# Waiting for the gated values block by block in the down projection

## The chip, the core and the metric

The kernel runs on one core of a Trainium2 chip. The metric is the device time of one execution in microseconds. Its reference is a median of three runs.

## The reference

One block with adaptive layer norm: a recurrent attention part with a gated MLP, then a mixture of experts. There are 1024 tokens (4 sequences of 256) of width D = 256. The part around the change is the MLP of the first half:

```
x1n = rmsnorm(x1, norm2_w)
mlp = gelu(x1n @ up1_W + up1_b) * (x1n @ up2_W + up2_b) @ down_W + down_b
return mlp + x1                       # times ga, plus x: this is x2
...
h = layernorm(x2) * (1 + cb) + sb
# router: logits = h @ gate_w, softmax, top 2 of 8 experts
# each expert: gelu(h @ w1[e] + b1[e]) @ w2[e] + b2[e], weighted and summed
```

The MLP is F = 768 wide. The product before `@ down_W`, the gated values, is called v here.

## The kernel before

Everything in the first half is held transposed: features on the 128 partitions, tokens along the free dimension. A tensor of D rows is two blocks of 128 (`KD` = 2), v is six (`KF` = 6). Tokens go in two halves of 512 (`hf` 0 and 1), which is one PSUM bank in float32. The five engines run streams of their own and meet at semaphores; there is no scheduler, the order on each engine is the order of the code. PSUM banks are handed out by a written-out list (`Order.take`); `begin` waits until the bank's former content is drained, `end` counts it as filled.

Products are made with float32 numbers split into a high and a low part, in three matmuls for each pair of blocks (`three`): hi x hi, weight hi x value lo, weight lo x value hi. So one `up` product has 2 x 3 matmuls and one `down` product 6 x 3. `up(hf, m)` makes the two `up` products for block m. Four engines then make the block m of v:

- ACT takes the GELU of `up1` into `g_tile` (`up_gelu`, L1014);
- DVE adds the bias to `up2` and multiplies, into `v_tile` (`v_of`, L1395);
- ACT copies it to `v_hi`, rounded to the format of the products (`v_hi_of`, L1009), and counts `v_hi_done`;
- POOL subtracts it from `v_tile`, which gives `v_lo` (L1652), and counts `v_lo_done`.

Both counts rise by one for each block, six for each half, in the order of the blocks. `v_tile` and `g_tile` have four buffers.

TensorE's order around the change, written out by hand:

```
up(0, 5); up(1, 0); down(0)
up(1, 1); up(1, 2); x2_to_tokens(0)
up(1, 3); up(1, 4); up(1, 5); xhat2_blocks(0)
down(1, [0]); logits(0); to_tokens("h2t", 0, hT); down(1, [1])
places(0); turn_weights(0); x2_to_tokens(1); second_biases(0); stay_busy
xhat2_blocks(1); logits(1); ...
```

`down(hf, dts)` makes the blocks `dts` of the output for a half. DVE turns `down` into x2 (`x2_of`, L1402 and L1408, tile `xT`); TensorE transposes it to tokens (`x2_to_tokens`, L699), DVE takes the layer norm (L1194 to L1205), TensorE transposes back (`xhat2_blocks`, L541), and DVE modulates into `hT` (L1259). `logits` (L718) multiplies this by the router's weights, DVE ranks the experts (`centre`, `choose`), TensorE counts places (`places`, L730 to L735), and DVE makes slots (`slots`). POOL then scatters the tokens' rows to the experts' lists in device memory, SP loads these lists, and the expert loop runs. `x2_of(1)` stands behind `slots(0)` in DVE's code.

In the rows below, L549 is the matmul in `product` (up and down products alike); those that read `v_hi` or `v_lo` belong to `down`.

Of the kernel before, what the change touches and what calls it, by code (L numbers as in the profile page):

```python
# [55 lines left out]
def adaln_block(nc, I, out):  # L56
# [10 lines left out]
    KD, KH, KF, KE = D // P, H // P, F // P, FE // P  # L67
# [112 lines left out]
    with ctx:  # L180
# [11 lines left out]
        def at(name, off, shape, dt=F32):  # L192
            return nc.alloc_sbuf_tensor_at(name, [P, *shape], dt, offset=off)
# [72 lines left out]
        v_hi, v_lo = at("v_hi", o_r1, [KF, T], F32R), at("v_lo", o_r1 + 3 * TB, [KF, T], F32R)  # L266
# [93 lines left out]
        v_hi_done, v_lo_done = sem("v_hi_done"), sem("v_lo_done")  # L360
# [29 lines left out]
        def three(m, n):  # L390

            return ((m[0], n[0]), (m[0], n[1]), (m[1], n[0]))
# [130 lines left out]
        def _(pe):  # L523
            def begin(key):
                b, _, need = order.at[key]
                if need:
                    pe.wait_ge(drained[b], need)
                return b, bank[b]

            def end(ins, b):  # L530
                ins.then_inc(filled[b], 1)
# [12 lines left out]
            def product(key, w, x, k, n=HT):  # L544

                b, ps = begin(key)
                for c in range(k):
                    for t, (l, r) in enumerate(three(w(c), x(c))):
                        ins = nc.tensor.matmul(ps[:, 0:n], l, r, start=(c == 0 and t == 0), stop=(c == k - 1 and t == 2))  # L549
                end(ins, b)  # L550
                return ins
# [59 lines left out]
            def wm(n, k):  # L611
                w = [x[:, n].rearrange("p (k n) -> p k n", k=k) for x in (wm_hi, wm_lo)]
                return lambda m: lambda c: tuple(x[:, c, m * P:(m + 1) * P] for x in w)

            def split_of(hi, lo, hf):
                return lambda c: (hi[:, c, hs[hf]], lo[:, c, hs[hf]])

            def wm_ready(n):
                pe.wait_ge(wm_hi_done, n)
                pe.wait_ge(wm_lo_done, n)  # L620
# [45 lines left out]
            b, ps = begin("gb")  # L666
            for k in range(KD):
                ins = nc.tensor.matmul(ps[0:B, 0:D], cT[:, k, :], wmod_gb[:, k, :], start=(k == 0), stop=(k == KD - 1))
# [15 lines left out]

            def down(hf, dts=range(KD)):
                wm_ready(3)
                pe.wait_ge(v_hi_done, KF * (hf + 1))
                pe.wait_ge(v_lo_done, KF * (hf + 1))
                for dt in dts:
                    product(("down", hf, dt), wm(2, KF)(dt), split_of(v_hi, v_lo, hf), KF)  # L690

            def to_tokens(key, hf, src):

# [72 lines left out]
            up(0, 5)  # L766
            up(1, 0)
            down(0)
            up(1, 1)
            up(1, 2)  # L770
# [3 lines left out]
            up(1, 5)  # L774
            xhat2_blocks(0)
            down(1, [0])
            logits(0)
            to_tokens("h2t", 0, hT)
            down(1, [1])
            places(0)  # L780
            turn_weights(0)
# [86 lines left out]
            with pe.If(ov == 0):  # L868
                for j in range(2):
                    b, _, need = order.at[("rest", j)]  # L870
# [871 lines left out]
```

## Time and profile before

| | us |
|---|---|
| median of three runs | 322.95 |
| lowest, highest | 319.52, 323.54 |
| the profiled execution | 318.49 |
| its span, first to last instruction | 316.7 |
| TensorE busy in it | 273.1 |
| DVE, ACT, POOL busy | 194.7, 180.4, 114.9 |

The profiled execution is one more execution, beside the three. Its time is 1.8 us more than its span; all rows are from it. Busy shares are averages over stages that differ, so they don't tell what a single wait is worth.

### The profile page before, as it was taken

How to read it: one execution, taken by the hardware profiler on the slowest of the kernel's cores; microseconds unless marked ns; L12 is line 12 of the kernel's file. 1: busy time of each engine (PE TensorE's matmuls, PEld its weight loads, DVE VectorE, ACT ScalarE, POOL GpSimd, SP SyncE). 2: the span in 40 equal slices, each digit the busy share in tenths (PEclk: the TensorE clock that was granted, in tenths of full speed). 3: DMA queues.
4: the chain of work that ended last, by engine and by line, in shares of the span. 5: the costliest groups of instructions: out<-in, count | busy, mean ns of one | idle time of the engine just before them, and what ended most of it. 6: DMA issues, size and time to landing. Idle time of an engine off the chain costs nothing.

```text
span 316.7 us, 4350 instructions
## 1 busy us (share of the span) xinstructions
PE 273.1 (86%) x1556; PEld 229.6 (72%) x1556; DVE 194.7 (61%) x450; ACT 180.4 (57%) x290; POOL 114.9 (36%) x97
## 2 busy tenths in 40 slices
PE   0799999958998999686959779999999999999780
PEld 0685446347686888565736669999999999999780
DVE  4766719739645276266495576767676767675520
ACT  5166589762497039251423669494949494949000
POOL 6000000000225033307227530656565656565651
PEclk9999999976999999996656999999999999999997
DMA  7960000000007564602104596393939393917231
GB/s 233 387 185 0 2 1 0 0 0 2 0 0 252 170 161 71 201 0 86 52 19 132 178 274 193 104 288 109 284 111 283 112 283 103 248 17 200 19 45 25
DMA packets 32726, 38.25 MB, mean 121 GB/s; under 512 B 7989, under 2 KB 28333, under 8 KB 32685
## 3 DMA queue, kind: packets, MB, share of 16 engines
q1 hardware_dynamic: 26816, 29.90, 30.0%
q0 software_dynamic: 4928, 7.44, 10.6%
q10 hardware_dynamic: 956, 0.59, 0.6%
q8 instruction: 14, 0.23, 0.3%
q14 instruction: 12, 0.09, 0.1%
HBM read 31.96 MB, written 8.90 MB: 129 GB/s over the span
## 4 chain that ended last, share of the span: by engine, by line
PE 70%; DVE 9%; ACT 8%; issue 6%; DMA 3%; POOL 2%; POOLq 0%; SPq 0%; ACTq 0%; DVEq 0%
PE bank L842 16%; PE bank L864 15%; PE bank L549 14%; PE bank L608 8%; PE bank L560 3%; DMA a_col<-in_L_attn_a_param 2%; PE bank L828 2%; PE bank L568 2%; PE bank L859 2%; PE bank L858 2%; PE bank L541 1%; DVE u L1303 1%; POOL v_lo L1652 1%; PE bank L699 1%; PE bank L753 1%
## 5 line engine op out<-in xcount | busy, mean ns | idle before, releaser
L1704 POOL DMA_INDIRECT out_x<-y_tok,meta x24 | 51.6, 2149 | 50.8 <-DVE y_tok L1576 44.6
L864 PE MATMUL bank<-w_hi,own 128*128 128x256 f32 x256 | 48.0, 286 | 1.8 <-DVE y_tok L1576 1.8
L842 PE MATMUL bank<-xe_hi,w_hi 128*128 128x320 f32 x128 | 39.7, 310 | 3.4 <-DVE xe_lo L1554 3.4
L864 PEld LDWEIGHTS bank<-w_hi,own 128*128 128x128 f32 x256 | 40.4, 191 | 2.4 <-issue 2.0
L1558 DVE TENSOR_TENSOR own<-own_raw,own 128x256 fp32r<-128x256 f32 x64 | 27.2, 425 | 23.5 <-ACT own L1134 18.9
L842 PE MATMUL bank<-xe_lo,w_hi 128*128 128x320 f32 x128 | 39.6, 309 | 0.0
L842 PE MATMUL bank<-xe_hi,w_lo 128*128 128x320 f32 x128 | 39.6, 309 | 0.0
L1128 ACT ACTIVATE own_raw<-bank,b1c 128x320 f32<-128x320 f32 x64 | 33.8, 529 | 8.5 <-PE bank L842 8.4
L864 PE MATMUL bank<-w_lo,own 128*128 128x256 f32 x128 | 36.2, 283 | 0.0
L1134 ACT ACTIVATE own<-own_raw 128x320 fp32r<-128x320 f32 x64 | 28.7, 461 | 0.0
L1695 POOL DMA_INDIRECT gb_rows<-gb_table,meta x24 | 24.4, 1016 | 9.4 <-issue 7.0
L842 PEld LDWEIGHTS bank<-xe_hi,w_hi 128*128 128x128 f32 x128 | 24.0, 188 | 3.7 <-issue 3.7
L864 PEld LDWEIGHTS bank<-w_lo,own 128*128 128x128 f32 x128 | 24.5, 191 | 0.0
L842 PEld LDWEIGHTS bank<-xe_lo,w_hi 128*128 128x128 f32 x128 | 24.0, 188 | 0.0
L842 PEld LDWEIGHTS bank<-xe_hi,w_lo 128*128 128x128 f32 x128 | 24.0, 188 | 0.0
L549 PE MATMUL bank<-n_hi,wm_hi 128*128 128x512 f32 x48 | 20.6, 429 | 3.1 <-DVE n_lo L1286 3.1
L1652 POOL TENSOR_TENSOR v_lo<-tmp,v_hi 128x512 fp32r<-128x512 f32 x6 | 7.7, 1286 | 40.7 <-ACT v_hi L1009 40.7
L1142 ACT ACTIVATE low_rows<-bank 64x256 f32<-64x256 f32 x8 | 3.0, 381 | 34.1 <-PE bank L859 34.1
L549 PE MATMUL bank<-n_lo,wm_hi 128*128 128x512 f32 x48 | 19.5, 407 | 0.0
L549 PE MATMUL bank<-n_hi,wm_lo 128*128 128x512 f32 x48 | 19.5, 405 | 0.0
L1576 DVE SCALAR_TENSOR_TENSOR y_tok<-bank,meta,gb_rows 128x256 f32<-128x256 f32 x16 | 7.7, 484 | 18.1 <-PE bank L864 17.5
L1488 DVE TENSOR_TENSOR w_lo<-e_raw,w_hi 128x2048 fp32r<-128x2048 f32 x8 | 18.6, 2327 | 0.0
(211 smaller groups left out, 614.2 us busy)
## 6 DMA issues: line engine op xcount, KB each, us to landing
e_raw<-in_L_ffn_w SPq DMA_DIRECT2D x16, 1024.0 KB
x_rows<-in_L_attn_x SPq DMA_DIRECT2D x1, 2560.0 KB
xe_tok<-x_rows SPq DMA_DIRECT2D x8, 256.0 KB
raw_m<-in_L_attn_up_W SPq DMA_DIRECT2D x2, 768.0 KB, 9.7
x_tok<-in_L_attn_x SPq DMA_DIRECT2D x2, 512.0 KB, 5.1
out_x<-x_tok SPq DMA_DIRECT2D x1, 1024.0 KB
wmod<-in_L_wmod SPq DMA_DIRECT2D x1, 768.0 KB, 12.1
raw_m<-in_L_attn_down_W SPq DMA_DIRECT2D x1, 768.0 KB, 13.4
```

Of the source, the lines that this page charges most:

```text
L549: ins = nc.tensor.matmul(ps[:, 0:n], l, r, start=(c == 0 and t == 0), stop=(c == k - 1 and t == 2))
L560: ins = nc.tensor.matmul(ps[:, j:j + 1], square[:, dt, hf * HT + j * P:hf * HT + (j + 1) * P], ones, start=(dt == 0 and j == 0), stop=(dt ...
L608: ins = nc.tensor.matmul(ps[:], raw_a[:, n, c, m * P:(m + 1) * P], x[:, c, hs[hf]], start=(c == 0), stop=(c == KD - 1))
L842: ins = nc.tensor.matmul(bank[b][:, 0:CAP], l, r, start=(c == 0 and t == 0), stop=(c == KD - 1 and t == 2))
L864: ins = nc.tensor.matmul(bank[b][0:n, 0:D], l, r, start=(c == 0 and t == 0), stop=(c == KE - 1 and t == 2))
L1128: nc.scalar.activation(own_raw[:, f % 4, :], bank[b][:, 0:CAP], ACT.Gelu, bias=b1c[:, g:g + 1]).then_inc(drained[b], 1)
L1134: nc.scalar.activation(own_hi[e % 2][:, f, :], own_raw[:, f % 4, :], ACT.Copy).then_inc(own_hi_done, 1)
L1488: nc.vector.tensor_tensor(w1_lo[e % 2][:], e_raw1[:].rearrange("p (k n) -> p k n", k=KD), w1_hi[e % 2][:].bitcast(F32), ALU.subtract).then ...
L1558: nc.vector.tensor_tensor(own_lo[e % 2][:, f, :], own_raw[:, f % 4, 0:whole], own_hi[e % 2][:, f, 0:whole].bitcast(F32), ALU.subtract)
L1652: nc.gpsimd.tensor_tensor(dst, whole, hi.bitcast(F32), ALU.subtract).then_inc(done, 1)
L1695: nc.gpsimd.indirect_dma_start(gb_rows[e % 2][0:n, k, :], None, gb_table, bass.IndirectOffsetOnAxis(ap=ids[0:n, e, k, E + 1:EXTRA], axis=0 ...
L1704: nc.gpsimd.indirect_dma_start(out_rows, bass.IndirectOffsetOnAxis(ap=ids[0:n, e, k, E:E + 1], axis=0), y_tok[e % 2][0:n, k, :], None, com ...
```

## The change

`down` no longer calls `product`. It writes the same matmuls out, in the same order, into the same banks, and the two waits on the gated values go into the loop over the six blocks: ahead of block c it waits for c + 1 blocks of the half, where it waited once for all six.

```diff
             def down(hf, dts=range(KD)):
                 wm_ready(3)
-                pe.wait_ge(v_hi_done, KF * (hf + 1))
-                pe.wait_ge(v_lo_done, KF * (hf + 1))
                 for dt in dts:
-                    product(("down", hf, dt), wm(2, KF)(dt), split_of(v_hi, v_lo, hf), KF)
+                    w, v = wm(2, KF)(dt), split_of(v_hi, v_lo, hf)
+                    b, ps = begin(("down", hf, dt))
+                    for c in range(KF):
+                        pe.wait_ge(v_hi_done, KF * hf + c + 1)
+                        pe.wait_ge(v_lo_done, KF * hf + c + 1)
+                        for t, (l, r) in enumerate(three(w(c), v(c))):
+                            ins = nc.tensor.matmul(ps[:], l, r, start=(c == 0 and t == 0), stop=(c == KF - 1 and t == 2))
+                    end(ins, b)
```

TensorE's stream from the last matmul of `up(1, 0)` into the first product of `down(0)`, before (a row is an instruction, with its bank, operands and the semaphores that it waits for; numbers behind names tell tiles apart):

```order
L549 MATMUL bank7<-n_hi_82,wm_lo_87 128x512
L549 MATMUL bank0<-v_hi_98,wm_hi_86 128x512 [waits v_lo_done,v_hi_done,bank_drained0,wm_lo_done,wm_hi_done]
L549 MATMUL bank0<-v_lo_99,wm_hi_86 128x512
L549 MATMUL bank0<-v_hi_98,wm_lo_87 128x512
L549 MATMUL bank0<-v_hi_98,wm_hi_86 128x512
L549 MATMUL bank0<-v_lo_99,wm_hi_86 128x512
```

The same place in the changed kernel:

```order
L549 MATMUL bank7<-n_hi_82,wm_lo_87 128x512
L694 MATMUL bank0<-v_hi_98,wm_hi_86 128x512 [waits v_hi_done,bank_drained0,v_lo_done,wm_lo_done,wm_hi_done]
L694 MATMUL bank0<-v_lo_99,wm_hi_86 128x512
L694 MATMUL bank0<-v_hi_98,wm_lo_87 128x512
L694 MATMUL bank0<-v_hi_98,wm_hi_86 128x512 [waits v_lo_done,v_hi_done]
L694 MATMUL bank0<-v_lo_99,wm_hi_86 128x512
```

The order stays. The first row's wait is for one block instead of six, and each further first matmul of three (five more in a product) has a pair of waits.

TensorE's stream from the transposes of `xhat2_blocks(0)` into `down(1, [0])`, before:

```order
L541 MATMUL bank6<-ident_49,xhat2_114 128x128 x3
L541 MATMUL bank7<-ident_49,xhat2_114 128x128 [waits bank_drained7]
L541 MATMUL bank7<-ident_49,xhat2_114 128x128 x3
L549 MATMUL bank0<-v_hi_98,wm_hi_86 128x512 [waits v_lo_done,v_hi_done,bank_drained0,wm_lo_done,wm_hi_done]
L549 MATMUL bank0<-v_lo_99,wm_hi_86 128x512
```

And now:

```order
L541 MATMUL bank6<-ident_49,xhat2_114 128x128 x3
L541 MATMUL bank7<-ident_49,xhat2_114 128x128 [waits bank_drained7]
L541 MATMUL bank7<-ident_49,xhat2_114 128x128 x3
L694 MATMUL bank0<-v_hi_98,wm_hi_86 128x512 [waits v_hi_done,bank_drained0,v_lo_done,wm_lo_done,wm_hi_done]
L694 MATMUL bank0<-v_lo_99,wm_hi_86 128x512
```

The same again: no row changes its place, and only the counts and places of the waits differ. The other engines' streams are the same as before.

## Rows read from the trace of the kernel before

**Rows 1.** The page: the span, TensorE's busy time, the chain's shares by engine

```profile
span 316.7 us, 4350 instructions
...
PE 273.1 (86%) x1556; PEld 229.6 (72%) x1556; DVE 194.7 (61%) x450; ACT 180.4 (57%) x290; POOL 114.9 (36%) x97
...
PE 70%; DVE 9%; ACT 8%; issue 6%; DMA 3%; POOL 2%; POOLq 0%; SPq 0%; ACTq 0%; DVEq 0%
```

**Rows 2.** TensorE's waits, 90 to 190 us: us in total, times, longest

```profile
PE bank L549 <- POOL v_lo L1652: 4.1, 2, 2.6
PE bank L699 <- DVE xT L1408: 3.8, 1, 3.8
```

**Rows 3.** TensorE in time around `down(0)`: start, us, what, [idle before <-releaser]

```profile
101.29 0.39 PE L549 MATMUL bank<-n_hi,wm_lo 128*128 128x512 f32 x1
103.17 0.47 PE L549 MATMUL bank<-v_hi,wm_hi 128*128 128x512 f32 x1 [1.50 <-POOL v_lo L1652]
103.48 0.40 PE L549 MATMUL bank<-v_lo,wm_hi 128*128 128x512 f32 x1
```

**Rows 4.** TensorE in time: two sets of transposes and what follows each

```profile
116.88 1.03 PE L699 MATMUL bank<-ident,xT 128*128 128x128 f32 x8
117.67 0.48 PE L549 MATMUL bank<-n_hi,wm_hi 128*128 128x512 f32 x1
...
125.93 1.03 PE L541 MATMUL bank<-ident,xhat 128*128 128x128 f32 x8
129.56 0.47 PE L549 MATMUL bank<-v_hi,wm_hi 128*128 128x512 f32 x1 [2.59 <-POOL v_lo L1652]
```

**Rows 5.** POOL in time: the last `v_lo` of either half

```profile
101.64 1.28 POOL L1652 TENSOR_TENSOR v_lo<-tmp,v_hi 128x512 fp32r<-128x512 f32 x1 [1.43 <-ACT v_hi L1009]
...
126.81 2.49 POOL L1652 TENSOR_TENSOR v_lo<-v_more,v_hi 128x512 fp32r<-128x512 f32 x2 [0.77 <-ACT v_hi L1009]
```

**Rows 6.** TensorE in time where `down(0)` gives way to `up(1, 1)`

```profile
111.21 0.39 PE L549 MATMUL bank<-v_hi,wm_lo 128*128 128x512 f32 x1
111.43 0.39 PE L549 MATMUL bank<-n_hi,wm_hi 128*128 128x512 f32 x1
111.66 0.39 PE L549 MATMUL bank<-n_lo,wm_hi 128*128 128x512 f32 x1
```

**Rows 7.** DVE in time, 126 to 152 us

```profile
126.92 1.89 DVE L1259 TENSOR_SCALAR hT<-bank,mod 128x256 f32<-128x256 f32 x4
135.64 0.19 DVE L1431 TENSOR_REDUCE small<-bank 128x4 f32<-128x32 f32 x1 [6.83 <-PE bank L718]
...
144.08 0.88 DVE L1408 SCALAR_TENSOR_TENSOR xT<-tmp,mod,xT 128x256 f32<-128x256 f32 x2
...
149.61 1.90 DVE L1205 TENSOR_SCALAR xhat<-bank,mv,rstd 128x256 f32<-128x256 f32 x4
```

**Rows 8.** TensorE in time, 133 to 154 us

```profile
133.76 1.84 PE L718 MATMUL bank<-gate_w,hT 128*128 128x8 f32 x16
...
145.02 1.97 PE L699 MATMUL bank<-ident,xT 128*128 128x128 f32 x8 [3.79 <-DVE xT L1408]
...
153.35 1.91 PE L541 MATMUL bank<-ident,xhat 128*128 128x128 f32 x8
```

**Rows 9.** Busy time by stretch; PEclk is the granted clock, then DMA

```profile
core 0: us, PE busy (x) PEld busy (x) DVE busy (x) ACT busy (x) POOL busy (x), PEclk, DMA share, GB/s
...
128.00:130.00 2.00, 0.44 (x2) 0.43 (x3) 0.81 (x2) 0.97 (x1) 1.30 (x2) 1.00 0.93 221
...
146.00:148.00 2.00, 2.00 (x8) 1.48 (x7) 0.91 (x3) 0.00 (x0) 1.69 (x2) 0.50 0.37 136
```

**Rows 10.** TensorE in time: two of nine matmuls at the lower clock

```profile
72.81 0.63 PE L549 MATMUL bank<-n_lo,wm_hi 128*128 128x512 f32 x1
...
76.22 0.63 PE L549 MATMUL bank<-n_hi,wm_hi 128*128 128x512 f32 x1
```

**Rows 11.** The tile `v_lo`: durations in ns, least, median, longest

```profile
L1652 POOL TENSOR_TENSOR v_lo<-v_more,v_hi x6: 1264/1296/1880, 92.0 to 128.0; 128x512 fp32r<-128x512 f32 x6
```

## The prediction

> **What bounds the kernel now.** I read the page first. TensorE is busy 86% of a 316.7 us span and 70% of the chain that ended last runs through it [rows 1]; the other engines matter where TensorE waits. So the second view is the list of TensorE's waits over the stretch that holds the change, 90 to 190 us. Its first line is the one that the change touches: 4.1 us, in two waits, for POOL's `v_lo` [rows 2]. The next is 3.8 us for DVE's `xT`, later in the same stretch.
>
> The third view is TensorE in order of time around the two waits. The last matmul of `up(1, 0)` starts at 101.29, the first of `down(0)` at 103.17 after 1.50 us of idleness [rows 3]. The transposes of `xhat2_blocks(0)` start at 125.93, the first matmul of `down(1, [0])` at 129.56 after 2.59 us of idleness [rows 4]. In both places the sixth block ends last: POOL makes the last `v_lo` of the first half from 101.64 to 102.92, and the last two of the second half from 126.81 to 129.30 [rows 5]. `down(1, [1])` and the second product of `down(0)` find everything done and wait for nothing.
>
> **What the change does, part by part.** It moves no instruction. It takes the wait for all six blocks away from the first matmul and puts a wait for one block ahead of each group of three.
>
> First gap. The matmuls before it are 0.23 us apart (111.21, 111.43, 111.66 in [rows 6]), so without a wait the first of `down(0)` starts at 101.29 + 0.23 = 101.52 instead of 103.17: 1.65 us. After a stop the first matmul also takes longer to be followed, 103.17 to 103.48 = 0.31 instead of 0.23 [rows 3]: 0.08 more. The sum is 1.73 us. Does a later block stop it? Five blocks of three are 15 x 0.23 = 3.4 us, so the sixth is wanted at 104.9 and was ready at 102.92. POOL works in order, so blocks one to five were ready before 101.64, where the sixth began; the first is wanted at 101.52 and had been ready long before. Nothing stops.
>
> Second gap. An equal set of eight transposes (116.88) is followed by a matmul after 0.79 us (117.67) [rows 4]. So the first matmul can start at 125.93 + 0.79 = 126.72 instead of 129.56: 2.84 us, with the slow first step in it on both sides. Blocks one to four were made before 126.81, when POOL began the last two; blocks five and six end at about 128.05 (half of POOL's 2.49 us) and 129.30 [rows 5]. The fifth is wanted 12 matmuls after 126.72, at 126.72 + 12 x 0.23 + 0.08 = 129.5, and the sixth at 130.2. From POOL's end to TensorE's start went 103.17 - 102.92 = 0.25 us [rows 3, 5]; with it they are there at 128.3 and 129.55, 1.2 and 0.65 us early. Again nothing stops, but the sixth has the smaller margin.
>
> The 20 new places with waits (five inside each of four products). The trace has no satisfied wait inside an accumulation, so I bound its price. Nearest row: where `down(0)` gives way to `up(1, 1)`, a matmul that waits for a bank, `n_hi` and `n_lo`, all long done, starts 0.22 us after the one before, as everywhere [rows 6]: price zero. The far end is a wait that works like a real stop: 0.25 us from the releaser's end to the start and 0.08 us of slow first step, 0.33 us. Below zero it can't be, since nothing is taken out there. I take zero, because that row is three satisfied waits ahead of the same kind of matmul.
>
> By the Trainium skill, "TensorE: Matmul & The Clock Gate" (Step-by-step: what each phase is for), an instruction may cost some 62 ns to dispatch when the sequencer decodes it in microcode; a second wait that needs an instruction of its own would by that, as an estimate, cost 20 x 0.062 = 1.2 us if nothing covered it, and nothing if the 0.23 us of each matmul covers it. The row on the three satisfied waits speaks for the cover.
>
> So TensorE is 1.73 us early from 101.5 on and 1.73 + 2.84 = **4.57 us** early from the second gap on.
>
> **Does it stay early?** Saved waiting is worth only what the next late thing leaves of it, so I followed the releasers.
> Between the gaps, ACT's GELUs, DVE's `v` blocks and POOL's `v_lo` all start on a bank that TensorE fills, and so move by 1.73 us with it.
> After the second gap the question is who moves by 1.73 us only. It is DVE's `hT` (L1259), which runs 126.92 to 128.81 and feeds `logits(0)` [rows 7]. It will end at 127.1; `logits(0)`, at 133.76 now [rows 8], will want it at 129.2: 2.1 us to spare.
> From `logits(0)` on there is one loop: DVE idles 6.83 us until it ends and starts at 135.64 [rows 7], works out ranks and, after `places(0)`, slots, then `x2_of(1)`, which ends at 144.96 and releases TensorE at 145.02 after its 3.79 us wait [rows 7, 8]. This longest wait of the stretch isn't shortened, but it isn't lengthened either: all of it, DVE's part too, starts from `logits(0)` and moves by 4.57 us. The second half's norm, logits, ranks, slots, scatters and the loads of gathered rows hang on it one after another, and the expert loop after them is a TensorE stream. What starts by itself, the weight loads of SP and the filling of `x_rows`, is over before it is wanted.
> Sum: 318.49 - 4.57 = 313.9 us for the profiled execution.
>
> **From there to the median.** The profiled execution (318.49) lies 4.5 us under the median (322.95), and the runs spread over 319.52 to 323.54. Taken from the median the sum gives 318.4; taken from the mean of all four times, 321.1, it gives 316.5. I take the middle, **317.5 us**. It is 1.7% under the median, and 2%, or 316.5 us, is about what a measurement of this kernel can tell from no change.
>
> **Rivals.**
> 1. *The clock moves too.* The granted clock was 1.00 (2.4 GHz) in 128 to 130, right after the 2.59 us gap, but 0.50 (1.2 GHz) in 146 to 148, after the 3.79 us wait [rows 9]. At the lower level matmuls of the same form are (76.22 - 72.81) / 8 = 0.43 us apart [rows 10], 0.20 more. Nine of them passed so there, which cost 1.8 us. If other executions of the kernel before lose that after the gap at 127, the changed kernel saves it too: gain 6.4, time 315.7 (counted, as in the rivals below, from 322.0, the middle base). The long stretch at the lower level after 145 can also shift: held at full clock, the transposes at 153.35 could start when DVE's `xhat` ends, 149.61 + 1.90 = 151.51, 1.8 us earlier [rows 7, 8]; held low for as much work again it costs about the same 1.8 us, and then the gain is 2.8 and the time 319.3. The Trainium skill, same page (The HAM clock gate), says that idleness takes the clock down and that the point at which it changes varies from run to run of one kernel; the row after the 3.79 us wait agrees, and no run here shows the variation yet.
> 2. *Only one gap pays.* `logits(0)` would have to meet a late `hT`, or the sixth block of the second half a late POOL: one `v_lo` took 1.88 us instead of 1.29 [rows 11]. If the second gain is lost, 1.73 stay: 320.3; if the first is, 2.84: 319.2. Against it stand the margins of 2.1 and 0.65 us.
> 3. *The waits break the stream, and the kernel gets slower.* If TensorE can't run on past a satisfied wait inside a product, each of the 20 places costs up to 0.33 us, 6.6 in all, against 4.57 gained: 2.0 us slower, 324.1. It decides from 4.57 / 20 = 0.23 us per place, one whole matmul. The row with three satisfied waits at 0.22 speaks against it.
> 4. *Nothing changes*, because the first block is in fact not released alone: 322. Counts rise in the order of the blocks on ACT and POOL, so I see no way for this.
>
> **How the numbers follow.** Both gaps close and all moves along: 0.66. Clock better 0.13, clock worse 0.08, one gap only 0.08, waits break the stream 0.03, nothing 0.02. The main case has about 1.6 us of spread around 317.5 from the base alone, so a quarter of it (0.17) lies under 316.5, with most of the better clock (0.11): faster by over 2% 0.28. Slower by over 2% needs 329.4, which only rival 3 with a bad clock nears: 0.02. The rest, 0.70, is within 2%. The range takes in both bases, the better clock on one side and the single gap on the other: 313.8 to 321.0.
>
> **What will show it.** Right: no wait for `v_lo` among TensorE's; the first matmul of `down(0)` 0.23 us after the last of `up(1, 0)`; that of `down(1, [0])` 0.79 us after the transposes; 0.23 us from matmul to matmul inside the products; the wait for `xT` still about 3.8 us, and all that follows, the gathered rows' transposes and the expert loop, 4.6 us earlier. Wrong: steps of 0.3 us or more at every third matmul; a new wait of `logits(0)` for `hT`; a wait for `xT` that has grown by what the gaps lost; the clock down in another place.

## The result, and the profile after

| | before | changed |
|---|---|---|
| median of 11 runs, us | 321.22 | 316.12 |
| lowest, highest | 317.50, 325.68 | 313.30, 319.74 |
| the profiled execution | 318.49 | 314.15 |
| its span | 316.7 | 312.3 |

The ratio is 0.9878 (95% interval 0.9837 to 0.9919), so the changed kernel is 1.2% faster, 3.9 us of 321; the interval leaves out 1, but the change is under the 2% that the prediction took as the least that can be told. The ratio leaves out executions in a second, slower state, which both kernels have; the medians, over all executions, are 5.1 us apart. The same kernel on another chip gave 0.9881 (0.9809 to 0.9953). The two profiled executions differ by 4.34 us.

TensorE's waits in the changed kernel, 85 to 190 us. The line for `v_lo` [rows 2] is gone and this one leads (lines of the code after `down` are 5 further on):

```profile
PE bank L704 <- DVE xT L1413: 3.8, 1, 3.8
```

TensorE in order of time: start, duration, what. These rows answer to [rows 3] and [rows 4]:

```profile
101.01 0.39 PE L549 MATMUL bank<-n_hi,wm_lo 128*128 128x512 f32 x1
101.24 0.39 PE L694 MATMUL bank<-v_hi,wm_hi 128*128 128x512 f32 x1
101.46 0.39 PE L694 MATMUL bank<-v_lo,wm_hi 128*128 128x512 f32 x1
101.69 0.39 PE L694 MATMUL bank<-v_hi,wm_lo 128*128 128x512 f32 x1
101.92 0.39 PE L694 MATMUL bank<-v_hi,wm_hi 128*128 128x512 f32 x1
...
109.40 0.39 PE L549 MATMUL bank<-n_hi,wm_hi 128*128 128x512 f32 x1
...
123.90 1.03 PE L541 MATMUL bank<-ident,xhat 128*128 128x128 f32 x8
124.69 0.48 PE L694 MATMUL bank<-v_hi,wm_hi 128*128 128x512 f32 x1
...
128.87 1.84 PE L723 MATMUL bank<-gate_w,hT 128*128 128x8 f32 x16
```

The first matmul of `down(0)` follows the last of `up(1, 0)` after 0.23 us, and the first of each three follows the one before at the same pace (101.69, 101.92). From the last matmul of `up(1, 0)` to the first of `up(1, 1)` it is now 109.40 - 101.01 = 8.39 us. This stretch is called A below. Before, it was 111.43 - 101.29 = 10.14 [rows 3, 6]. From the transposes of `xhat2_blocks(0)` to `logits(0)`, stretch B, it is 128.87 - 123.90 = 4.97, where it was 7.83 [rows 4, 8]. The rest of the difference in starts, 0.28 us, was there before `down(0)`.

POOL still makes its last two `v_lo` beside it, and DVE's `hT` ends at 126.78, 2.1 us ahead of `logits(0)`:

```profile
124.78 2.54 POOL L1657 TENSOR_TENSOR v_lo<-v_more,v_hi 128x512 fp32r<-128x512 f32 x2 [0.77 <-ACT v_hi L1014]
```

```profile
124.89 1.89 DVE L1264 TENSOR_SCALAR hT<-bank,mod 128x256 f32<-128x256 f32 x4
130.75 0.19 DVE L1436 TENSOR_REDUCE small<-bank 128x4 f32<-128x32 f32 x1 [3.97 <-PE bank L723]
```

Who now waits for whom changed in one way: DVE's idleness before the ranking fell from 6.83 [rows 7] to 3.97 us, because `logits(0)` comes sooner after `hT`. TensorE's wait for `xT` is still 3.79 us, as in [rows 8]:

```profile
140.12 1.09 PE L704 MATMUL bank<-ident,xT 128*128 128x128 f32 x8 [3.79 <-DVE xT L1413]
...
147.48 1.35 PE L541 MATMUL bank<-ident,xhat 128*128 128x128 f32 x8
```

Up to here the changed kernel is 145.02 - 140.12 = 4.90 us ahead, of which 0.28 are older: 4.62. Then the clock takes part. The granted clock is the number behind POOL's column. Three stretches of the changed kernel, the first two to set beside [rows 9]:

```profile
144.00:146.00 2.00, 2.00 (x5) 1.16 (x5) 1.74 (x4) 1.14 (x3) 1.39 (x3) 0.50 0.20 72
148.00:150.00 2.00, 1.25 (x11) 1.04 (x10) 1.57 (x4) 0.00 (x0) 0.21 (x1) 0.97 0.19 68
...
172.00:174.00 2.00, 2.00 (x10) 2.00 (x9) 1.49 (x1) 0.60 (x2) 2.00 (x1) 0.50 0.88 270
```

And one of the kernel before, in its first expert:

```profile
178.00:180.00 2.00, 2.00 (x16) 2.00 (x15) 1.20 (x1) 1.24 (x3) 1.85 (x1) 1.00 0.81 221
```

In both kernels it fell to 0.50 after the wait for `xT`, but in the changed kernel it was back at 1.00 at about 148, during the transposes at 147.48, which took 1.35 us where they had taken 1.91 [rows 8]. TensorE was 153.35 - 147.48 = 5.87 us ahead there and at the first matmul of the expert loop 177.26 - 171.55 = 5.71. Then the clock of the changed kernel fell once more, at 172, in the first expert, where the kernel before had 1.00 (178 to 180). The matmuls of the first expert stand 0.15 us apart at full clock and 0.27 here:

```profile
171.55 0.38 PE L847 MATMUL bank<-xe_hi,w_hi 128*128 128x320 f32 x1 [1.25 <-DVE xe_lo L1559]
171.77 0.31 PE L847 MATMUL bank<-xe_lo,w_hi 128*128 128x320 f32 x1
...
173.97 0.47 PE L847 MATMUL bank<-xe_lo,w_hi 128*128 128x320 f32 x1
174.23 0.47 PE L847 MATMUL bank<-xe_hi,w_lo 128*128 128x320 f32 x1
```

The first matmul of the first expert's second layer started at 195.92 before and starts at 191.60 now: 4.32 us ahead. So this fall cost 5.71 - 4.32 = 1.4 us, and from there to the end the kernels run alike: the profiled executions differ by the 4.34 us above. Neither of the two shifts of the clock belongs to the change for certain: a second trace of the changed kernel, among the experiments, has them elsewhere.

### The profile page after: what moved, and what is told of

Same layout as the page of the kernel before. It is cut to its first block and busy times, and to the rows that moved or that the text cites. A ratio compares the mean times of both kernels' runs of the same rounds, so it can differ in the third digit from the quotient of the medians.

```text
span 312.3 us, 4371 instructions
## 1 busy us (share of the span) xinstructions
PE 272.5 (87%) x1556; PEld 229.8 (74%) x1556; DVE 194.6 (62%) x450; ACT 180.6 (58%) x290; POOL 115.6 (37%) x97
## 5 line engine op out<-in xcount | busy, mean ns | idle before, releaser
L847 PE MATMUL bank<-xe_hi,w_hi 128*128 128x320 f32 x128 | 40.4, 315 | 3.3 <-DVE xe_lo L1559 3.3
L847 PE MATMUL bank<-xe_hi,w_lo 128*128 128x320 f32 x128 | 40.3, 315 | 0.0
L847 PEld LDWEIGHTS bank<-xe_lo,w_hi 128*128 128x128 f32 x128 | 24.7, 193 | 0.0
```

The costliest lines, as they stand in the source:

```text
L847: ins = nc.tensor.matmul(bank[b][:, 0:CAP], l, r, start=(c == 0 and t == 0), stop=(c == KD - 1 and t == 2))
```

## Experiments

Executions of one kernel lie up to 2.6% apart (317.50 to 325.68 before), so what each half of a change of 1.2% gives is read from stretches A and B, which end before the first large wait of TensorE that is common to both, and the ratios stand beside them.

### One gap at a time

Waits by block in the first half only:

```diff
-                        pe.wait_ge(v_hi_done, KF * hf + c + 1)
-                        pe.wait_ge(v_lo_done, KF * hf + c + 1)
+                        pe.wait_ge(v_hi_done, KF * hf + (KF if hf else c + 1))
+                        pe.wait_ge(v_lo_done, KF * hf + (KF if hf else c + 1))
```

> Waits by block in the first half only; down(1, ...) waits for all six again, ahead of each block. Two stretches are read from the trace, which the clock after 140 us can't touch: A, from the last matmul of up(1, 0) to the first of up(1, 1) (10.14 us before, 8.39 in the changed kernel), and B, from the transposes of xhat2_blocks(0) to logits(0) (7.83 before, 4.97 in the changed kernel). Theory (each gap pays for itself, the rest moves along): A 8.4, B 7.8 or a little more, the wait for v_lo at 2.6 us, and the time 1.7 us under the kernel before. Rival (only one of the gaps pays, the other is taken by a later wait): if this one pays nothing, the time is that of before; if it pays all, 4 to 5 us under it.

And in the second half only (`c + 1 if hf else KF`):

> Waits by block in the second half only. Theory: A 10.1 us, B 5.0, one wait for v_lo of 1.5 us left, the time 2.8 us under the kernel before; with the first half's alone (1.7) it adds up to the whole change. Rival (only one gap pays): 0, or the whole 4 to 5 us.

| | A | B | ratio to before (95%) |
|---|---|---|---|
| before | 10.14 | 7.83 | |
| first half only | 8.39 | 9.29 | 0.9963 (0.9902 to 1.0024) |
| second half only | 10.03 | 4.97 | 0.9941 (0.9889 to 0.9993) |
| both (the change) | 8.39 | 4.97 | 0.9878 (0.9837 to 0.9919) |

A and B fall as expected, each with its own waits alone; the one wait left in the second run is the first gap's:

```profile
PE bank L694 <- POOL v_lo L1657: 1.4, 1, 1.4
```

The ratios are 0.4% and 0.6%, together 1.0%, of the same size as the 1.2% of both; by their intervals alone the first could be nothing. That one gap pays all or nothing is refuted by the stretches.

B of the first run is an unplanned finding. It is 1.5 us longer than in the kernel before, though this half's waits are those of before. TensorE around the gap, and the granted clock:

```profile
127.15 0.66 PE L694 MATMUL bank<-v_hi,wm_hi 128*128 128x512 f32 x1 [2.48 <-POOL v_lo L1657]
127.62 0.63 PE L694 MATMUL bank<-v_lo,wm_hi 128*128 128x512 f32 x1
128.04 0.63 PE L694 MATMUL bank<-v_hi,wm_lo 128*128 128x512 f32 x1
...
132.93 1.29 PE L723 MATMUL bank<-gate_w,hT 128*128 128x8 f32 x11
```

```profile
124.00:126.00 2.00, 0.67 (x7) 0.43 (x4) 2.00 (x5) 1.68 (x3) 1.48 (x2) 1.00 0.01 2
126.00:128.00 2.00, 0.85 (x2) 0.73 (x3) 0.52 (x2) 0.68 (x1) 1.01 (x1) 0.82 0.38 139
128.00:130.00 2.00, 2.00 (x6) 1.57 (x5) 0.00 (x0) 0.00 (x0) 0.00 (x0) 0.50 0.89 236
```

The clock fell just as the gap ended, at about 127.3: the next eight steps are 0.42 to 0.47 us where [rows 6] has 0.23, and B grew by 9.29 - 7.83 = 1.46 us. So a gap of this length, which left the clock alone in the first trace [rows 9], doesn't always. In an execution where it falls there, closing the gap would give back 9.29 - 4.97 = 4.32 us instead of 2.86. Four traces here have the second gap (2.59 us in the kernel before; 2.48, 2.48 and 2.60 us in this run and two below), and the clock fell behind it in this one alone; four profiles don't tell how often it happens.

### The price of the waits

The code of the changed kernel with the counts of before (`KF * (hf + 1)` ahead of every block): all the waits and no early start.

> The changed kernel's code with the counts of before: a pair of waits ahead of each block, but for all six, so that no block starts early; 21 more instructions that only wait. Theory (a satisfied wait inside a product is free): A 10.1 us, B 7.8, 0.23 us from matmul to matmul inside down, the time of before within 0.5 us. Rival (the waits break the stream): 0.06 to 0.33 us at each of the 20 places, A and B longer by 0.6 to 3.3 us (ten places) and 0.3 to 1.7 us (five places), the time 1.2 to 6.6 us over before.

Measured: ratio 1.0001 (0.9947 to 1.0055), A 10.06, B 7.70, no longer than before. TensorE at the first gap; the fourth row has a pair of waits ahead of it, and the step to it is the 0.23 us of the others:

```profile
102.57 0.47 PE L694 MATMUL bank<-v_hi,wm_hi 128*128 128x512 f32 x1 [1.39 <-POOL v_lo L1657]
102.88 0.40 PE L694 MATMUL bank<-v_lo,wm_hi 128*128 128x512 f32 x1
103.11 0.40 PE L694 MATMUL bank<-v_hi,wm_lo 128*128 128x512 f32 x1
103.34 0.40 PE L694 MATMUL bank<-v_hi,wm_hi 128*128 128x512 f32 x1
```

Next, one pair ahead of each of the 72 matmuls, and four pairs ahead of each:

```diff
-                        pe.wait_ge(v_hi_done, KF * hf + c + 1)
-                        pe.wait_ge(v_lo_done, KF * hf + c + 1)
                         for t, (l, r) in enumerate(three(w(c), v(c))):
+                            for _ in range(4):          # 1 in the other kernel
+                                pe.wait_ge(v_hi_done, KF * hf + c + 1)
+                                pe.wait_ge(v_lo_done, KF * hf + c + 1)
```

> The changed kernel with four pairs of waits, eight satisfied waits, ahead of each of the 72 matmuls of down, three instructions that only wait between any two matmuls. Theory (waits are handled while the matmul before runs, so they are free as long as they fit in 0.23 us): either 0.23 us from matmul to matmul still, or, if three are too many, a pace that is even and longer, which gives the price of one. Rival (each wait stops the stream): every step 0.2 us or more longer, 72 x 0.2 = 14 us over the changed kernel.

> The changed kernel with one pair of waits ahead of each of the 72 matmuls, one instruction that only waits between any two. With three of them the pace was 0.45 us after nine matmuls at 0.23, as if a supply had run out. Theory (a wait instruction costs TensorE's sequencer time, which a stock of instructions read ahead covers as long as it lasts): if all five instructions of a step cost the same, one is 0.09 us, and a step of three 0.27 us, once the stock is used up; stretch A (8.39) at most 1.5 us longer. If the waits are cheaper than matmuls, the pace stays at 0.23. Rival (a wait between matmuls stops the stream whatever their number): 0.45 us here too.

| | instructions that only wait, per matmul of `down` | A | B | step inside `down` |
|---|---|---|---|---|
| changed | 1/3 | 8.39 | 4.97 | 0.23 |
| a pair for each matmul | 1 | 8.39 | 4.97 | 0.23 |
| four pairs for each | 4 | 13.93 | 8.28 | 0.23, then 0.45 |

The middle column is counted in the traces. TensorE's queue (PEldq) has 147 + 144 instructions that only wait (EVENT_SEMAPHORE) from the two wait lines of the kernel with four pairs, 72 + 3 in the kernel with one pair and 24 in the changed kernel, for 72 matmuls: 4 x 72 and three more, 72 and three more, 72 / 3. So the two expectations above are wrong in saying three: four pairs make four.

```profile
L694 PEldq EVENT_SEMAPHORE  x147: 51/51/51, 99.4 to 147.8; - x147
...
L693 PEldq EVENT_SEMAPHORE  x144: 51/51/51, 99.5 to 147.7; - x144
```

One such instruction for each matmul is free: A and B are those of the changed kernel (its ratio, from two executions, is 0.9854, 0.9753 to 0.9955). Four are not, and their trace shows how: the first twelve matmuls of `down(0)` still follow at 0.23 us (the expectation above says nine), then at 0.44 to 0.51.

```profile
104.52 0.39 PE L695 MATMUL bank<-v_hi,wm_hi 128*128 128x512 f32 x1
104.75 0.39 PE L695 MATMUL bank<-v_lo,wm_hi 128*128 128x512 f32 x1
104.97 0.43 PE L695 MATMUL bank<-v_hi,wm_lo 128*128 128x512 f32 x1
105.48 0.47 PE L695 MATMUL bank<-v_hi,wm_hi 128*128 128x512 f32 x1
105.92 0.47 PE L695 MATMUL bank<-v_lo,wm_hi 128*128 128x512 f32 x1
```

Of the two cases written down for the single pair the second holds: no step of 0.27 shows, the pace of 0.23 stayed. The rival, a stop at every wait, is refuted by both: the single pair costs nothing, and with four there is a run of fast steps first.

The supply that runs out can be seen in the same trace. The instructions that only wait run in the queue ahead of the matmuls that they stand before, 0.11 to 0.13 us apart. By the first matmul of `down(0)`, at 102.48, 28 of them had run, enough for seven matmuls, and the wait for the first matmul had run 2.7 us before it. From there the queue needs four of them, 0.44 us, for each matmul of 0.23 us, so the lead shrinks by 0.21 us a step: as an estimate it lasts 2.7 / 0.21 = 13 matmuls, and twelve were seen. After that the last wait runs only 0.1 us ahead of its matmul and the step is the queue's, 0.44 us. In the kernel with one pair the waits need 0.13 us of each 0.23 and stay 1.9 us or more ahead all through `down(0)`. As an estimate from the same rows, two instructions for each matmul would need 0.22 to 0.25 us, about the whole step; two and three weren't tried.

The kernel with four pairs took 329.5 us, ratio 1.030 (1.0197 to 1.0403), 4.3% over the changed one's 0.9878: the same waits, only more of them.

### The clock in and after the next wait

Fourteen matmuls that nobody reads, in TensorE's wait for `xT`:

```diff
     order.take(("cwT", 0))
+    order.take(("busy", 0), drains=0)
     take_x2t(1)
...
             turn_weights(0)
+            pe.wait_ge(w1_hi_done, 1)
+            stay_busy(("busy", 0), w1_hi[0].rearrange("p k n -> p (k n)"), 14)
             x2_to_tokens(1)
```

> The changed kernel with 14 idle matmuls (128x512, a result that nobody reads) into a spare bank, in TensorE's longest wait, the 3.8 us for xT, so that the engine isn't idle before 140 us. They take 14 x 0.23 = 3.2 us of 3.8. Theory (the clock falls because of this wait): the granted clock stays at 1.00 up to 148 us, the b2 products and the busy matmuls take half as long (3.67 and 2.93 us now), the transposes of xhat2_blocks(1) start when xhat is done, and the time falls by 1 to 2 us. Rival (the clock falls for another cause, or is not on the path): the time stays. Second rival (the filling delays the transposes of x2): up to 1 us slower.

Measured: median 314.64, ratio 0.9792 (0.9728 to 0.9857). TensorE from the filling on:

```profile
136.35 3.43 PE L634 MATMUL bank<-w_hi 128*128 128x512 f32 x14
140.40 1.09 PE L705 MATMUL bank<-ident,xT 128*128 128x128 f32 x8 [0.61 <-DVE xT L1416]
141.42 1.99 PE L759 MATMUL bank<-b_row,cwT 8*128 8x256 f32 x8
143.34 1.66 PE L634 MATMUL bank<-w_hi 128*128 128x512 f32 x6
146.11 1.09 PE L542 MATMUL bank<-ident,xhat 128*128 128x128 f32 x8 [1.11 <-DVEq L1432]
```

The wait is 0.61 us, and the b2 products take 1.99 us (3.67 in the changed kernel), the busy matmuls 1.66 (2.93). From the transposes of x2 to those of `xhat` it is 146.11 - 140.40 = 5.71 us, where the changed kernel has 147.48 - 140.12 = 7.36 and the kernel before 8.33 [rows 8]. The filling delayed nothing (its 140.40 is 11.27 us after `logits(0)`, as without it). All fourteen traces side by side bear out that the fall after 140 comes of this wait: in the nine where it lasts 3.79 or 3.80 us the clock fell every time, in the wait or shortly behind it, and the stretch took 7.18 to 8.33 us; in the five where it lasts 1.18 us or less the stretch took 5.65 to 5.72 us in four and 6.02 us in one. At the first matmul of the first expert 1.1 us of the gain is left (41.61 us after `logits(0)` instead of 42.68). In the whole time it is not shown: the ratio is 0.9% under the changed kernel's with overlapping intervals, and the profiled execution took 314.74 us against 314.15.

Twenty-four instead of sixteen such unread matmuls ahead of the expert loop (the last argument of `stay_busy(("busy", 2), ...)`):

> The changed kernel with 24 instead of 16 idle matmuls ahead of the expert loop, where TensorE sat idle 2.19 us for the gathered rows and the clock was at 0.50 from 172 to about 175. The eight more take 1.8 us at full clock. Theory (that fall of the clock cost the changed kernel's profiled execution 1.4 us of what it had gained by 170): no fall at 172, time 0.5 to 1.4 us under the changed kernel in executions that have it. Rival: the filling delays the turn of the gathered rows where the clock is low at 161, 0.5 us or more slower.

Measured: ratio 0.983 (0.9777 to 0.9882), not to be told from the changed kernel. Its clock:

```profile
168.00:170.00 2.00, 2.00 (x10) 1.50 (x8) 0.00 (x0) 0.00 (x0) 1.16 (x2) 1.00 0.91 285
...
172.00:174.00 2.00, 0.76 (x3) 0.79 (x4) 1.92 (x3) 1.72 (x2) 1.41 (x2) 0.83 0.28 44
174.00:176.00 2.00, 2.00 (x10) 2.00 (x9) 1.19 (x1) 0.53 (x1) 2.00 (x1) 0.50 0.87 271
```

The expectation was wrong in its theory. The clock was up at 168 to 170 and still fell at about 173 and stayed low at 174 to 176, so the filling ahead of the transposes doesn't prevent it. The wait for the gathered rows was 0.59 us here, where the changed kernel has 2.19. Between their transposes and the first expert's matmuls TensorE waits again, 1.25 us for `xe_lo`, which the filling doesn't cover. That wait alone doesn't decide it either: it is there in all fourteen traces (1.25 to 1.34 us), and the clock fell around it (from 0.3 us before it to 1 us behind it) in eight of them. The cause stays open.

### What is late next

TensorE's longest wait in the stretch is for `xT`: in DVE's code `x2_of(1)` stands behind the ranking and the slots.

```diff
-            def x2_of(hf):
+            def x2_of(hf, dts=range(KD)):
-                for dt in range(KD):
+                for dt in dts:
...
-            centre(0)
-            choose(0)
-            slots(0)
             until_drained(("xr", 1, 0))
             until_drained(("xr", 1, 1))
-            x2_of(1)
+            x2_of(1, [0])
+            centre(0)
+            choose(0)
+            x2_of(1, [1])
+            slots(0)
```

> The changed kernel with DVE's x2_of(1) taken apart: its first block runs ahead of centre(0), while DVE waits for logits(0), and its second ahead of slots(0). Theory (what is late next is DVE's order, x2_of(1) queued behind the ranking and the slots): the wait for xT falls from 3.8 to about 1 us, all that follows comes 2.5 to 3 us earlier; slots(0) and POOL's first scatters come 1.6 us later, which costs nothing, since POOL idles 9.3 us before the second scatters. Rival (the time is bound by the scatters or by the clock): under 1 us.

Measured: median 309.13, ratio 0.9624 (0.956 to 0.9687), the fastest of all kernels here. DVE makes the first block while it waits for `logits(0)` and the second directly behind the ranking, and starts the slots at 137.76:

```profile
129.55 0.75 DVE L1407 SCALAR_TENSOR_TENSOR tmp<-bank,cols,hT 128x512 f32<-128x512 f32 x1 [2.39 <-PE bank L694]
...
136.18 0.75 DVE L1407 SCALAR_TENSOR_TENSOR tmp<-bank,cols,hT 128x512 f32<-128x512 f32 x1 [0.91 <-PE bank L694]
136.97 0.88 DVE L1413 SCALAR_TENSOR_TENSOR xT<-tmp,mod,xT 128x256 f32<-128x256 f32 x2
137.76 0.18 DVE L1482 TENSOR_TENSOR rt<-bank,slot_base 128x32 f32<-128x32 f32 x1
```

TensorE's wait for `xT` is 1.18 us, and the transposes of `xhat` follow those of x2 after 5.72 us, about as with the filling (5.71):

```profile
137.90 1.09 PE L704 MATMUL bank<-ident,xT 128*128 128x128 f32 x8 [1.18 <-DVE xT L1413]
...
143.62 1.09 PE L541 MATMUL bank<-ident,xhat 128*128 128x128 f32 x8 [1.11 <-DVEq L1429]
```

So the shorter wait gives twice: 137.90 - 129.25 = 8.65 us from `logits(0)` to the transposes, where the changed kernel has 11.25, is 2.6 us; and with 1.18 us of idleness the clock of this trace stayed up through the next stretch, 7.36 - 5.72 = 1.6 us. That makes 4.2 us. A part was given back in this execution: the clock was at 1.00 in 142 to 144 and at 0.50 in 146 to 148,

```profile
142.00:144.00 2.00, 0.89 (x6) 0.45 (x5) 1.52 (x4) 1.29 (x3) 1.44 (x2) 1.00 0.31 113
...
146.00:148.00 2.00, 2.00 (x11) 2.00 (x11) 0.21 (x1) 0.00 (x0) 1.62 (x2) 0.50 0.37 136
```

so `logits(1)` took 3.55 us instead of 1.92, and from `logits(0)` to the first matmul of the first expert it was 168.67 - 129.25 = 39.42 us, where the changed kernel has 171.55 - 128.87 = 42.68: 3.3 us left. The medians differ by more than either number (316.12 and 309.13, ratios 0.9878 and 0.9624, 8 us by the ratios). The profiled execution took 311.25, four of the other five less. Where those gained more wasn't seen, since only one is profiled, and it stays open.

The same edit on the kernel before:

> DVE's early x2_of(1) on the kernel before, without waits by block. Theory (the two edits take different waits and add up): a wait for xT of 1.2 us, both waits for v_lo still there (4.1 us), stretches A and B as before, and the time under the kernel before by what the early x2_of(1) gained on the changed kernel, some 6 to 8 us, and over the run with both edits by 4 to 5. Rival (the early x2_of(1) pays only because the waits by block brought everything forward): 2 us or less under the kernel before.

Measured: median 314.44, ratio 0.9857 (0.979 to 0.9924); wait for `xT` 1.18 us, both waits for `v_lo` there (4.1 us), A 10.14, B 7.82. The edits take different waits. Their ratios multiply to 0.9878 x 0.9857 = 0.9737, with an interval of about 0.966 to 0.982 as an estimate from the two; the run with both has 0.9624 (0.956 to 0.9687). The two meet at the edge, so whether the edits give more together than one by one can't be told. Alone on the kernel before, the edit gave 4.6 us by the ratio, less than the 6 to 8 expected. In its trace the transposes of x2 come 2.6 us sooner after `logits(0)` (8.65 for 11.26), and those of `xhat` follow after 6.02 us instead of 8.33. The clock did not stay up here: it fell at about 144.4, in the b2 products, though the wait ahead of them was the same 1.18 us as in the run above.

The changed kernel beside it on the same chip:

> The changed kernel once more, for a comparison on the same chip with the two next. 4 to 6 us under the kernel before, ratio 0.980 to 0.990.

Measured: 0.9881 (0.9809 to 0.9953), A 8.39, B 4.97, as the first time. But the profiled execution took 317.24 us, 3.1 more than the first trace of the same kernel. The difference is the clock: `logits(0)` starts at 128.88 (128.87 the first time), the transposes of `xhat` at 148.22 (147.48), the first expert at 172.02 (171.55) and its second layer at 194.69 (191.60). The clock was low in 148 to 150, where the first trace has 0.97, and from 172 to 178 it was low for longer:

```profile
148.00:150.00 2.00, 2.00 (x9) 1.52 (x8) 0.68 (x2) 0.48 (x1) 0.22 (x1) 0.50 0.19 68
```

So executions of one kernel differ by this much through the clock alone, and what it did in one pair of traces can't be put down to the change.

All three edits together:

> The three edits together, on the changed kernel. If they add up: 4 to 6 us under the changed kernel. If the early x2_of(1) removes the wait that the idle matmuls fill, these now delay the transposes: 14 x 0.23 = 3.2 us less about 1 us of wait left, so only 1 to 2 us under the changed kernel.

Measured: median 311.48, ratio 0.9718 (0.9669 to 0.9766). The matmuls now overfill, as in the second case: the transposes of x2 start at 139.48, 10.50 us after `logits(0)` instead of 8.65, without a wait. The time misses that case all the same: it is 4.6 us under the changed kernel's median (316.12), not 1 to 2, and 2.4 us over the early `x2_of(1)` alone. Without the filling in the middle, but with the longer one at the end:

> Early x2_of(1) on the changed kernel, with the 24 idle matmuls ahead of the expert loop but none in the wait for xT, which delayed the transposes by 1.6 us when both were there. Theory: as fast as the early x2_of(1) alone (309.1) or up to 1.4 us faster, since the clock falls less often at the start of the expert loop. Rival (the longer filling meets the gathered rows): up to 1 us slower.

Measured: median 310.87, ratio 0.9691 (0.9623 to 0.9758), not to be told from the early `x2_of(1)` alone (0.956 to 0.9687). The early `x2_of(1)` alone ran on another chip, the changed kernel's second run (0.9881) on this one. TensorE had no wait for the gathered rows left there: the filling met them.

## Why the prediction was right

- **The first gap, 1.73 us.** A fell by 10.14 - 8.39 = 1.75 us. Right, and with the first half's waits alone it fell by the same.
- **The second gap, 2.84 us.** B fell by 7.83 - 4.97 = 2.86 us. Right; the first matmul follows the transposes after 124.69 - 123.90 = 0.79 us, as taken from the equal set.
- **No block comes too late.** Right. The sixth `v_lo` ended at 124.78 + 2.54 = 127.32, and its first matmul started at 128.18, 0.86 us later; I had 0.65 with 0.25 us for the signal taken off.
- **The waits cost nothing.** Right, and not only argued: 21 more wait instructions without any early start gave 1.0001, and even one for each matmul left A and B as they were. The rival that they break the stream needed 0.23 us for each place. The reason that I gave held too: the 0.23 us of a matmul covers them. My price for one, 0.062 us, was a matmul's figure carried over to a wait and too low: the traces show 0.11 to 0.13 us in the queue, still less than the 0.23 us of a matmul. Four for each matmul are too many.
- **The rest moves along.** Right up to the wait for `xT`: 4.62 us ahead, the wait unchanged at 3.79, `hT` 2.1 us early as worked out.
- **The clock.** Held as a rival with a price of 1.8 us either way, and it did act in the profiled executions, but in both directions: 1.0 us more in hand at the transposes of `xhat` (5.87 against 4.90), 1.4 us lost at the first expert. What is left, 4.34 us, is near the sum of 4.57 partly by such a balance, and that is luck: the second trace of the same kernel, with the same A and B, took 3.1 us more. The price itself was too low. I let the transposes start when `xhat` ended, but `xhat` comes sooner too, since the transposes that feed it then take 1.09 us instead of 1.97: with the wait filled the stretch fell from 8.33 to 5.71, 2.6 us. That an execution can lose its clock at the second gap, which I took for possible, the run with the first half's waits showed, at 1.46 us where I had 1.8.
- **The base.** 317.5 was 1.4 us over the measured 316.12. The sum against the profiled execution was 313.9 and that execution took 314.15. Of the 1.4 us, 0.8 are the base: the median before was 321.22 over eleven runs, near the mean of 321.1 that I had and not the 322.95 of three, and halfway between the two (322.0) was too high. The rest is that the medians moved by 5.1 us. Measured by the ratio the gain is 3.9 us (2.6 to 5.2), which holds 4.57 but doesn't show it to better than about 1 us. The two stretches show it directly: 1.75 + 2.86 = 4.61.

## What to carry to other kernels

A wait for all parts ahead of a product that uses them one after another costs the making of the last parts whenever the consumer arrives early; put it ahead of each part, after comparing, part by part, when it is made and when it is wanted. Look at what idleness does to the clock before and after: a wait of 2.5 us cost 1.5 us more than itself in one trace of four. Read a small gain from the stretches that it touches, since the clock alone moved the whole by 3.1 us between two traces of one kernel. And read what is late next, in whose code order it stands: here moving `x2_of(1)` on DVE gave about as much as the change (0.9857 alone, 0.9878), and it could be had beside it.

## What the runs showed of the hardware

- TensorE takes one instruction that only waits (its count long reached) for each 128x512 matmul at full clock without losing anything of the 0.23 us step; four make it 0.44 to 0.51 us, after twelve matmuls at the old pace.
- Such instructions run 0.11 to 0.13 us apart, ahead of the matmuls that they stand before: 2.7 us ahead at the start of `down(0)` with four for each matmul, 0.1 us once the lead was used up.
- The granted clock fell to 0.50 right behind a gap of 2.48 us in one execution and stayed at 1.00 after gaps of 2.48, 2.59 and 2.60 us in the same place in three others. In the wait of 3.8 us for `xT` or shortly behind it, it fell in all nine traces that have this wait. After waits of 1.18 us or less there it stayed up through the next stretch in four traces and fell within it in a fifth (6.02 us instead of 5.65 to 5.72).
- It also fell at the start of the expert loop in eight of fourteen traces, where no single wait was long: 2.19 us, six transposes and 1.25 us in the changed kernel, 0.59 and 1.25 us with more filling ahead. What decides it stays open.
